# Four-stage attention and expert kernel: the last attention batch in its own bank with its projection behind the third chunk, channel attention one group later, and the last chunk in two halves

## The chip, the cores and the metric

The kernel runs on one core of a Trainium2 chip, in one launch. The metric is the device time of the whole launch in microseconds (us), lower is better. The engines are named as the profile names them: PE is TensorE, PEld its weight loads, DVE VectorE, ACT ScalarE, POOL GpSimd, SP SyncE, which here issues nearly all DMAs.

## The reference

`x` and `ctx` are (8, 128, 128) float32: 8 batches of 128 tokens and 128 channels. Four residual stages follow each other; `ln` is a layer norm without weights.

```python
x = x + channel_attention(ln(x), ctx, ctx)      # 4 heads of 32 channels, "global" + "local" scaling
x = x + expert_attention(ln(x))                 # 16 experts mix q, k, v; causal softmax; 16 experts project out
x = x + cross_attention(ctx, ln(x), ctx)        # 16 heads of 8: softmax(q k^T) v @ Wc.T + bc
x = x + expert_ffn(ln(x))                       # 8 experts, top 2, hidden 176, plus a shared branch of 352
```

The last stage, in which most of the change lies, is

```python
router = xf @ Wg;  top_logits, idx = top_k(router, 2);  w = scatter(softmax(top_logits))
h = silu(einsum('tc,ech->eth', xf, W1)) * einsum('tc,ech->eth', xf, W2)
y = einsum('eth,ehc,te->tc', h, W3, w) + (silu(xf @ Ws1) * (xf @ Ws2)) @ Ws3
```

## The kernel before, in words

Everything is laid out for 128 partitions. Each engine has one program in which a loop over a step number `s` calls small functions at steps written out by hand (`at_mix`, `at_score`, `at_att`, `at_tail`, `at_first`, `at_once`); within an engine the instructions run in exactly that order, and between engines semaphores order them. A PSUM bank is `PB[i]`, 128 x 512 float32; who may write a bank next is settled by waits too.

**Channel attention** works on halves of four batches. DVE computes scores and softmax, turns the heads (`turn_heads`, L1004) into a block-diagonal matrix `bd`, and PE multiplies it with the values (`attend_channels`, L1386, 8 products, 16 machine instructions). For the second half this lies inside the loop of the second stage: PE runs `turn_keys` (L1377), `spread` (L1472, the routing weights of four experts spread over the partitions) and `project` (L1488, four experts' q, k, v); DVE makes the scaled inputs `hm` (`scale_hidden`, L1099). After `attend_channels(1)` come DVE's statistics (L1011), ACT's `take_x1` (L594), and on SP the first loads of routing weights (L416), which wait for `att_ready`. ACT copies q, k, v out (L651, L652) before PE can turn them (L1498).

**Cross attention** (`at_att`) goes batch by batch: scores turned (L1596), exponential on ACT (L700), product with the values (`attend3`, L1609, 32 instructions into PB[3]), ACT takes it (`take_y`, L711), PE turns it (`turn_y`, L1616, into PB[3]), DVE divides (`divide`, L1162 and L1165), PE turns it back (`turn_divided`, L1622, PB[3]), ACT takes `yT` (L717), PE adds x and projects (`bring_x` L1631, `project_c` L1635, into PB[5]), DVE takes statistics (L1169), ACT takes x (`take_x3`, L721), POOL computes the reciprocal root (L488), DVE normalises (L881). All batches share PB[3], so `attend3(b)` waits for `yT_ready` of batch b-1.

**Router.** The 1024 tokens are two halves of 512. For the first half PE turns x (L1645) and multiplies with Wg (L1654) in PB[6]; DVE finds the two best (L1177 to L1196) and splits the weights into three bf16 parts (`three_parts`, L915 to L919); `turn_w` turns them (L1660, L1665); ACT takes them (`take_wT`, L757 and L759); SP stores them (L442) and loads them spread over partitions (L452) for the chunks that are not spread by PE.

**Expert chunks.** The 1760 hidden rows of the last stage (352 shared and 8 x 176) are 14 chunks of 128 rows, the last of 96, for each half of the tokens: k = 0 to 27. `up(k)` is six products of 512 columns (L1677: high and low parts of x and of two weights), ACT applies silu (L769, or L765 in place), DVE multiplies (`hidden`: L1219 for shared chunks, L1221 and L1223 for the three whose routing weights PE spreads by L1714, L1212 and L1215 for the others), ACT makes the high part (`high_hidden`, L746), POOL the low part (`split_hidden`, L533; the last two chunks on DVE, L1231), and `down(k)` is three products (L1733), the third of which needs the low part. Chunks 2, 3 and 4 are the ones spread by PE. `down(0)` is followed by eight instructions that add x (L1739). `result` (L773) and the store on SP (L457) end each half.

Around the change the hand-written places are: `attend_channels(1)` at step 16, before the step's `spread` and `project`; `attend3(7)`, `turn_y(7)`, `turn_divided(7)`, `bring_x(7)`, `project_c(7)` and `turn_w(0)` between `up(0)`, `up(1)` and `up(2)`; and the spread of chunk 2 inside `up(2)`.

## Time and profile before

| | us |
|---|---|
| median of 3 runs | 235.6 (233.77 to 235.94) |
| profiled execution, its own time | 234.7 |
| its span | 232.9 |
| PE busy | 209.8 (90%) |
| DVE busy | 166.4 (71%) |
| ACT busy | 112.0 (48%) |
| POOL busy | 95.1 (41%) |

The span runs from the first to the last instruction that the profile shows, and 1.8 us of the profiled execution's time lie around it. Times in the rows are in us from the span's start. The ends of matmuls are modelled, so durations of PE rows overlap; what a PE group costs is read here from the start of one group to the start of the next.

### The profile page before, as it was taken

The page shows a single profiled execution, that of the slowest core. Times are in us where ns is not written, and L with a number is a line of the kernel's source. Part 1 is how long each engine was busy: PE and PEld are TensorE (multiplying, and loading weights), DVE is VectorE, ACT ScalarE, POOL GpSimd, SP SyncE. Part 2 cuts the span into 40 slices and gives each one's busy share as a digit, 9 for nine tenths or more (in the row PEclk, how much of TensorE's full clock was granted, in tenths as well). Part 3 has the DMA queues.
Part 4 walks back from the last instruction along what each step waited for, and adds up shares of the span by engine and source line. Part 5 has one row for each costly group of instructions (what it writes and reads, how often), then busy time and mean ns, then how long its engine had stood idle before and what let it go on. Part 6 is the DMA issues. An engine that isn't in the chain of part 4 may idle for free.

```text
span 232.9 us, 5017 instructions
## 1 busy us (share of the span) xinstructions
PE 209.8 (90%) x1784; PEld 176.6 (76%) x1785; DVE 166.4 (71%) x495; ACT 112.0 (48%) x259; POOL 95.1 (41%) x127
## 2 busy tenths in 40 slices
PE   0199867899999999999999999998899999999994
PEld 0156546899999999998779888876677887778871
DVE  3498798659979889967686787864865687267653
ACT  0424543232244554422355867778354645645552
POOL 7142300160076999920321021231345755647660
PEclk9999999999999999999999999999999999999998
DMA  5998000298089955030210000000022320144401
GB/s 181 354 413 245 3 6 0 85 298 161 28 245 260 270 146 146 14 80 0 57 37 3 3 0 3 0 4 0 3 91 57 127 91 3 66 166 156 135 24 45
DMA packets 19256, 23.33 MB, mean 100 GB/s; under 512 B 1792, under 2 KB 12192, under 8 KB 19104
## 3 DMA queue, kind: packets, MB, share of 16 engines
q1 hardware_dynamic: 18896, 22.94, 32.7%
q8 instruction: 14, 0.23, 0.4%
q10 hardware_dynamic: 336, 0.08, 0.2%
q14 instruction: 10, 0.08, 0.1%
HBM read 22.39 MB, written 0.62 MB: 99 GB/s over the span
## 4 chain that ended last, share of the span: by engine, by line
PE 80%; DVE 9%; ACT 3%; DMA 3%; issue 2%; ACTq 1%; POOL 0%; DVEq 0%
PE psum L1677 17%; PE psum L1488 17%; PE psum L1733 8%; PE psum L1531 6%; PE psum L1596 3%; PE psum L1569 3%; PE psum L1609 3%; DMA kv<-kv_dram 3%; PE psum L1386 2%; PE psum L1342 2%; PE psum L1506 1%; PE psum L1554 1%; PE psum L1616 1%; PE psum L1521 1%; PE psum L1582 1%
## 5 line engine op out<-in xcount | busy, mean ns | idle before, releaser
L488 POOL TENSOR_TENSOR rstd<-ve,m 128x1 f32<-128x1 f32 (+1 forms) x20 | 14.2, 712 | 94.0 <-DVE ve L872 93.9
L1488 PE MATMUL psum<-wqkv,hm 128*128 128x192 f32 x256 | 46.4, 328 | 0.0
L533 POOL TENSOR_TENSOR qs<-hm,qs 128x512 fp32r<-128x512 f32 (+1 forms) x26 | 33.9, 1305 | 22.5 <-ACT qs L746 22.4
L1488 PEld LDWEIGHTS psum<-wqkv,hm 128*128 128x128 f32 x256 | 41.1, 190 | 0.1
L1144 DVE TENSOR_REDUCE negm<-psum 128x8 f32<-128x1024 f32 x16 | 19.5, 1222 | 7.7 <-PE psum L1569 7.2
L1733 PE MATMUL psum<-qs,wdhi 128*128 128x512 f32 (+1 forms) x56 | 21.8, 401 | 0.1
L1212 DVE TENSOR_TENSOR hm<-hm,psum 128x512 f32<-128x512 f32 x19 | 13.0, 686 | 11.4 <-PE psum L1677 5.5
L1099 DVE TENSOR_TENSOR hm<-xn2T,exT 128x512 f32<-128x512 f32 x24 | 19.3, 805 | 0.1
L746 ACT ACTIVATE qs<-hm 128x512 fp32r<-128x512 f32 (+1 forms) x28 | 17.5, 625 | 3.9 <-DVE hm L1215 2.5
L700 ACT ACTIVATE exT<-psum 128x1024 f32<-128x1024 f32 x16 | 16.4, 1023 | 5.6 <-PE psum L1596 5.1
L765 ACT ACTIVATE psum<-psum 128x512 f32<-128x512 f32 x19 | 11.1, 582 | 16.3 <-PE psum L1677 16.1
L1531 PE MATMUL psum<-wo,mixT 128*128 128x128 f32 x128 | 15.7, 276 | 0.1
L1531 PEld LDWEIGHTS psum<-wo,mixT 128*128 128x128 f32 x128 | 15.0, 192 | 0.3 <-issue 0.2
L1215 DVE TENSOR_TENSOR hm<-hm,psum 128x512 f32<-128x512 f32 x19 | 13.0, 687 | 2.0
L1733 PEld LDWEIGHTS psum<-qs,wdhi 128*128 128x128 f32 (+1 forms) x56 | 10.5, 188 | 3.3 <-DVE qs L1231 0.9
L1131 DVE TENSOR_TENSOR mixT<-aT,rwm 128x1024 f32<-128x1024 f32 x8 | 10.8, 1350 | 2.8 <-issue 2.6
L1677 PE MATMUL psum<-x4hi,wahi 128*128 128x512 f32 (+1 forms) x28 | 12.0, 430 | 0.2
L1596 PE MATMUL psum<-qs,ks 32*128 32x128 f32 x128 | 10.5, 281 | 1.0 <-ACT qs L705 0.9
L1733 PE MATMUL psum<-qs,wdlo 128*128 128x512 f32 (+1 forms) x28 | 11.1, 397 | 0.0
L1677 PE MATMUL psum<-x4lo,wahi 128*128 128x512 f32 (+1 forms) x28 | 11.1, 396 | 0.0
L1677 PE MATMUL psum<-x4lo,wbhi 128*128 128x512 f32 (+1 forms) x28 | 11.0, 394 | 0.0
L1677 PE MATMUL psum<-x4hi,walo 128*128 128x512 f32 (+1 forms) x28 | 11.0, 394 | 0.0
(237 smaller groups left out, 488.2 us busy)
## 6 DMA issues: line engine op xcount, KB each, us to landing
exT<-rw_rows SPq DMA_DIRECT2D x24, 256.0 KB, 4.4
rwm<-rw_rows SPq DMA_DIRECT2D x16, 256.0 KB, 5.0
hm<-ww_rows SPq DMA_DIRECT2D x7, 256.0 KB, 3.2
wqkv<-wqkv_dram SPq DMA_DIRECT2D x1, 1536.0 KB, 10.6
hm<-ww_rows SPq DMA_DIRECT2D x4, 224.0 KB, 2.9
wa<-wa_dram SPq DMA_DIRECT2D x1, 880.0 KB, 13.3
wb<-wb_dram SPq DMA_DIRECT2D x1, 880.0 KB, 13.4
wdn<-wdn_dram SPq DMA_DIRECT2D x1, 832.0 KB, 15.0
```

The costliest lines, as they stand in the source:

```text
L488: nc.gpsimd.tensor_tensor(dst, src, m16[:, 0:src.shape[1]], ALU.pow).then_inc(signal, 1)
L533: return nc.gpsimd.tensor_tensor(dst, src, hi.bitcast(F32), ALU.subtract)
L700: nc.scalar.activation(exT[:, b % 2, 2 * p:2 * p + 2, :], turned_pair, ACT.Exp).then_inc(ex_ready, 1)
L746: nc.scalar.activation(hhi[0:n, k % 3, :], hid[0:n, k % 3, :], ACT.Copy).then_inc(hhi_ready, 1)
L1099: V.tensor_tensor(hm[:, b % 2, 4 * q:4 * q + 4, :], bc(xn2T[:, b, :], 1, 4), weights, ALU.mult).then_inc(hm_ready, 1)
L1144: V.tensor_reduce(negm[:, b % 2, 2 * p:2 * p + 2, :], score_pair.rearrange("p j (g k) -> p j g k", g=4), AX.X, ALU.max, negate=True).then_ ...
L1212: V.tensor_tensor(hid[:, k % 3, :], ww[:, r % 3, :], bank, ALU.mult).then_inc(prod_ready, 1)
L1488: last = mm(bank[:, 0:3 * HD], hm[:, b % 2, e, :], wqkv[:, e, :], start=(e == 0), stop=(e == E0 - 1))
L1531: last = mm(PB[5][:, 0:C], mixT[:, r, :], wo[:, r, :], start=(r == 0), stop=(r == E0 // 2 - 1))
L1596: last = mm(PB[turned_score_bank(j)][:, T * g:T * g + T], ks[quarter(j), b, g, :], qs[quarter(j), b, g, :], start=True, stop=True)
L1677: last = mm(bank[0:n, :], w[:, c0:c0 + n], x[:, cols4], start=(j == 0), stop=(j == 2))
L1733: last = mm(bank[:, :], w[0:n, ch, :], h[0:n, k % 3, :], start=(ch == 0 and j == 0), stop=(ch == NCH - 1 and j == 2))
```

## The change

It has three parts, with no change in what is computed.

1. **Channel attention.** `attend_channels(1)` moves on PE from step 16 to step 18, which puts it behind the step's `spread` and `project`.
2. **Last attention batch.** Batch 7 of the cross attention uses PB[6] in place of PB[3] for its product, its two turnings and their readers. `attend3(7)` waits for `rt_used` (the first router half has been read out of PB[6]) in place of `yT_ready` of batch 6; `turn_w(0)`, which also writes PB[6], gets a wait for `yT_ready` of batch 7. `bring_x(7)`, `project_c(7)` and `turn_w(0)` move behind `up(2)`. The spreading product of chunk 2 leaves `up(2)` and stands as `spread_first` behind `down(0)` and its x products, with a semaphore `first_spread` for which DVE's second multiplication of chunk 2 waits. On ACT the high part of chunk 0 moves behind silu of chunk 1, and `take_x3(7)` ahead of `take_wT(0)`.
3. **Last chunk.** Silu, multiplication and high part of k = 27 are done in a left and a right half of 256 columns; the left low part is on POOL (new), the right one on DVE behind the low part of k = 26; `down(26)` leaves its third product to `down(27)`, which is now five products: four of high parts by halves, the third product of 26, and two half products of low parts. On ACT the high part of k = 26 moves ahead of silu of k = 27.

PE around the channel attention. L1386 (L1433 in the changed kernel) is the attention, L1472/L1519 the spreading, L1488/L1535 the projection, L1377/L1424 the turning of keys. Before:

```order
94 L1377 MATMUL psum<-ident,ksp 128x128 x4
95 L1386 MATMUL psum<-exT 128x128 x8
96 L1472 MATMUL psum<-partsT,sel 128x128 x4
97 L1488 MATMUL psum<-wqkv,hm 128x192 x4
98 L1377 MATMUL psum<-ident,ksp 128x128 x4
```

The same place in the changed kernel:

```order
94 L1424 MATMUL psum<-ident,ksp 128x128 x4
95 L1519 MATMUL psum<-partsT,sel 128x128 x4
96 L1535 MATMUL psum<-wqkv,hm 128x192 x4
97 L1433 MATMUL psum<-exT 128x128 x8
98 L1424 MATMUL psum<-ident,ksp 128x128 x4
```

One spreading and one projection now stand ahead of the attention; nothing else moves there.

ACT around the last attention batch. `qs<-hm` is a high part, `hm<-psum` silu, `xr` take_x3, `yT` take_yT, `ysb` take_y. Before:

```order
182 L711 ACTIVATE ysb<-psum 128x512 [waits z_ps,pv_done]
183 L746 ACTIVATE qs<-hm 128x512 [waits hid_ready]
184 L769 ACTIVATE hm<-psum 128x512 [waits up_ready]
185 L721 ACTIVATE xr<-psum 128x128 [waits x3_stats]
186 L717 ACTIVATE yT<-psum 128x128 [waits c_ready,yT_ps]
187 L746 ACTIVATE qs<-hm 128x512 [waits hid_ready]
188 L757 ACTIVATE wwT<-psum 32x128 [waits wwT_ps,wT_ps]
189 L759 ACTIVATE wT<-psum 128x512
190 L721 ACTIVATE xr<-psum 128x128 [waits x3_stats]
```

In the changed kernel:

```order
182 L733 ACTIVATE ysb<-psum 128x512 [waits z_ps,pv_done]
183 L803 ACTIVATE hm<-psum 128x512 [waits up_ready]
184 L776 ACTIVATE qs<-hm 128x512 [waits hid_ready]
185 L743 ACTIVATE xr<-psum 128x128 [waits x3_stats]
186 L739 ACTIVATE yT<-psum 128x128 [waits c_ready,yT_ps]
187 L776 ACTIVATE qs<-hm 128x512 [waits hid_ready]
188 L743 ACTIVATE xr<-psum 128x128 [waits x3_stats]
189 L787 ACTIVATE wwT<-psum 32x128 [waits wwT_ps,wT_ps]
190 L789 ACTIVATE wT<-psum 128x512
```

The first high part changes places with the silu behind it, and the last x stands ahead of the two copies of the routing weights.

ACT at the end of the program, before:

```order
243 L746 ACTIVATE qs<-hm 128x512
244 L769 ACTIVATE hm<-psum 96x512
245 L746 ACTIVATE qs<-hm 128x512
246 L746 ACTIVATE qs<-hm 96x512
247 L773 ACTIVATE xna<-psum 128x512
```

And in the changed kernel:

```order
243 L776 ACTIVATE qs<-hm 128x512 x2
244 L800 ACTIVATE hm<-psum 96x256
245 L801 ACTIVATE hm<-psum 96x256
246 L772 ACTIVATE qs<-hm 96x256
247 L774 ACTIVATE qs<-hm 96x256
248 L807 ACTIVATE xna<-psum 128x512
```

The high part of k = 26 goes ahead of the silu of k = 27, and both steps of k = 27 are in halves.

The diff, cut to its core:

```diff
+            def split_left(k):
+                pool.wait_ge(hhi_half, 1)
+                pool.wait_ge(down_done, k - 2)
+                low_part(hlo[0:n, k % 3, LEFT], hid[0:n, k % 3, LEFT], hhi[0:n, k % 3, LEFT]).then_inc(hlo_half, 1)
...
-                nc.scalar.activation(ysb[:, :, :].rearrange("p g t -> p (g t)"), PB[3][:, :], ACT.Copy).then_inc(y_ready, 1)
+                nc.scalar.activation(ysb[:, :, :].rearrange("p g t -> p (g t)"), PB[y_bank(b)][:, :], ACT.Copy).then_inc(y_ready, 1)
...
+                if is_last(k):
+                    nc.scalar.activation(gated[0:n, k % 2, LEFT], PB[gate_bank(k)][0:n, LEFT], ACT.Silu).then_inc(gated_half, 1)
+                    nc.scalar.activation(gated[0:n, k % 2, RIGHT], PB[gate_bank(k)][0:n, RIGHT], ACT.Silu).then_inc(gated_ready, 1)
+                    return
...
+                if n_routed(k) == 1:
+                    dve.wait_ge(first_spread, 1)
                 V.tensor_tensor(hid[:, k % 3, :], hid[:, k % 3, :], PB[3 if n_routed(k) % 2 == 1 else 4][:, :], ALU.mult).then_inc(hid_ready, 1)
...
+                if is_last(k):
+                    V.tensor_tensor(hlo[0:n, k % 3, RIGHT], hid[0:n, k % 3, RIGHT], hhi[0:n, k % 3, RIGHT].bitcast(F32), ALU.subtract).then_inc(hlo_ready, 1)
+                    return
...
                 if b == 0:
                     pe.wait_ge(aT_ready, NB)
+                elif b == NB - 1:
+                    pe.wait_ge(rt_used, 1)
                 else:
                     pe.wait_ge(yT_ready, b)
...
             def turn_w(hf):
+                if hf == 0:
+                    pe.wait_ge(yT_ready, NB)
...
+                    pe.wait_ge(hhi_half, 1)
+                    part(wdhi, hhi, LEFT, False)
+                    part(wdlo, hhi, LEFT, False)
+                    pe.wait_ge(hhi_ready, k + 1)
+                    part(wdhi, hhi, RIGHT, False)
+                    part(wdlo, hhi, RIGHT, False)
+                    pe.wait_ge(hlo_ready, k)
+                    mm(bank[:, :], wdhi[0:128, ch - 1, :], hlo[0:128, (k - 1) % 3, :], start=False, stop=False).then_inc(down_done, 1)
+                    pe.wait_ge(hlo_half, 1)
+                    part(wdhi, hlo, LEFT, False)
+                    pe.wait_ge(hlo_ready, k + 1)
+                    part(wdhi, hlo, RIGHT, True).then_inc(down_done, 1)
+                    return
...
-                if s == at_once(16):
+                if s == at_once(18):
                     attend_channels(1)
...
-                    if s == at_att(b, 62):
+                    if s == at_last(b, 62, 73):
                         bring_x(b)
...
-                    if s == at_tail(hf, 128, 176):
+                    if s == at_tail(hf, 137, 176):
                         turn_w(hf)
+                if s == at_once(LAST_W):
+                    spread_first()
```

## Rows read from the trace of the kernel before

**Rows 1.** The page: busy time of each engine, and the chain that ended last.

```profile
PE 209.8 (90%) x1784; PEld 176.6 (76%) x1785; DVE 166.4 (71%) x495; ACT 112.0 (48%) x259; POOL 95.1 (41%) x127
PE 80%; DVE 9%; ACT 3%; DMA 3%; issue 2%; ACTq 1%; POOL 0%; DVEq 0%
```

**Rows 2.** Waits of PE, the one that is touched first: us in total, times, longest.

```profile
PE psum L1386 <- DVE exT L1004: 1.4, 1, 1.4
```

**Rows 3.** Timeline, 37 to 51 us: start, duration, engine, line [idle before <- releaser].

```profile
41.45 2.05 PE L1386 MATMUL psum<-exT 128*128 128x128 f32 x16 [1.38 <-DVE exT L1004]
43.34 0.39 PE L1472 MATMUL psum<-partsT,sel 128*128 128x128 bf16 x4
...
43.59 3.67 SPq L416 DMA_DIRECT2D exT<-rw_rows  x8
...
44.36 0.88 DVE L1011 BATCH_NORM_STATS2 st<-psum 128x6 f32<-128x128 f32 x4
...
44.91 0.60 PE L1377 MATMUL psum<-ident,ksp 128*128 128x128 f32 x4
...
47.68 0.29 ACT L652 ACTIVATE v<-psum 128x128 f32<-128x128 f32 x1
...
48.51 0.27 PE L1498 MATMUL psum<-ident,qk 128*64 128x128 f32 x1
...
50.19 0.68 DVE L1099 TENSOR_TENSOR hm<-xn2T,exT 128x512 f32<-128x512 f32 x1
```

**Rows 4.** Landing times of the second stage's routing-weight transfers (tile rw_rows).

```profile
DMA to landing us min/median/max: 1.8/4.5/8.1
```

**Rows 5.** Timeline, 162 to 174 us.

```profile
163.34 1.08 PE L1609 MATMUL psum<-exT,vm 128*32 128x128 f32 x32 [1.01 <-ACT yT L717]
...
166.40 1.30 POOL L533 TENSOR_TENSOR qs<-hm,qs 128x512 fp32r<-128x512 f32 x1
...
166.53 1.22 DVE L916 TENSOR_TENSOR ga<-rww,wparts 128x32 f32<-128x32 f32 x1
...
167.89 0.28 ACT L717 ACTIVATE yT<-psum 128x128 f32<-128x128 f32 x1
...
168.06 0.49 PE L1631 MATMUL psum<-xr,ident 128*128 128x128 f32 x2 [0.74 <-ACT xr L721]
...
170.68 0.47 PE L1677 MATMUL psum<-x4hi,wahi 128*128 128x512 f32 x1
...
172.15 0.39 PE L1714 MATMUL psum<-wT,selw 128*128 128x512 bf16 x1
...
172.21 0.69 DVE L1223 TENSOR_TENSOR hm<-hm,psum 128x512 f32<-128x512 f32 x1
...
172.81 0.34 DVE L881 TENSOR_SCALAR xnb<-xr,mv,rstd 128x128 f32<-128x128 f32 x1
...
173.87 0.48 PE L1677 MATMUL psum<-x4hi,wahi 128*128 128x512 f32 x1
```

**Rows 6.** Timeline of the end, 226 to 230 us.

```profile
226.40 0.60 ACT L769 ACTIVATE hm<-psum 96x512 f32<-96x512 f32 x1 [0.96 <-PE psum L1677]
...
227.10 0.68 DVE L1219 TENSOR_TENSOR hm<-hm,psum 96x512 f32<-96x512 f32 x1 [1.25 <-ACT hm L769]
...
227.70 1.50 DVE L1231 TENSOR_TENSOR qs<-hm,qs 128x512 fp32r<-128x512 f32 x2
227.81 0.63 ACT L746 ACTIVATE qs<-hm 96x512 fp32r<-96x512 f32 x1 [0.30 <-DVE hm L1219]
...
229.79 0.60 ACT L773 ACTIVATE xna<-psum 128x512 f32<-128x512 f32 x1 [1.35 <-PE psum L1733]
```

**Rows 7.** Timeline, 67 to 69 us: POOL's subtractions beside a DVE product.

```profile
67.58 0.45 POOL L533 TENSOR_TENSOR wdlo<-wdn,wdhi 128x128 fp32r<-128x128 f32 x1
67.58 1.53 DVE L1131 TENSOR_TENSOR mixT<-aT,rwm 128x1024 f32<-128x1024 f32 x1 [1.11 <-issue]
...
68.16 1.26 POOL L533 TENSOR_TENSOR walo<-wa,wahi 128x128 fp32r<-128x128 f32 x1
```

More of the change, by code:

```diff
@@ L39 @@
 W4 = 13
+LAST_W = 474
 SLOT = 8
@@ L262, in build @@
         wparts_ready = sem("wparts_ready"); wT_ps = sem("wT_ps"); wT_ready = sem("wT_ready")
-        up_ready = sem("up_ready"); gated_ready = sem("gated_ready"); prod_ready = sem("prod_ready")
+        up_ready = sem("up_ready"); first_spread = sem("first_spread"); gated_ready = sem("gated_ready"); prod_ready = sem("prod_ready")
         hid_ready = sem("hid_ready"); hhi_ready = sem("hhi_ready"); hlo_ready = sem("hlo_ready")
@@ L278, in chunk_rows, with is_last @@
             return min(128, RUP - 128 * ch)
+        LEFT, RIGHT = slice(0, 256), slice(256, 512)
+        def is_last(k):
+            return k == 2 * NCH - 1
         def is_routed(k):
@@ L321, in at_att, with at_last, y_bank @@
             return SLOT * (Q3 + 2 * b) + u - ATT_EARLY[b]
+        def at_last(b, u, v):
+            return at_att(b, v if b == NB - 1 else u)
+        def y_bank(b):
+            return 6 if b == NB - 1 else 3
         def at_once(u):
@@ L574, in _ @@
                     split_hidden(s // SLOT - F4 - 1)
+                if s == LAST - 1:
+                    split_left(2 * NCH - 1)
         @block.scalar
@@ L716, in take_yT @@
                     act.wait_ge(c_ready, b - 1)
-                nc.scalar.activation(yT[:, b % 2, :], PB[3][:, 0:T], ACT.Copy).then_inc(yT_ready, 1)
+                nc.scalar.activation(yT[:, b % 2, :], PB[y_bank(b)][:, 0:T], ACT.Copy).then_inc(yT_ready, 1)
             def take_x3(b):
@@ L742, in high_hidden @@
                 n = chunk_rows(k % NCH)
-                act.wait_ge(hid_ready, k + 1)
+                if is_last(k):
+                    act.wait_ge(hid_half, 1)
+                else:
+                    act.wait_ge(hid_ready, k + 1)
                 if k >= 3:
                     act.wait_ge(down_done, k - 2)
+                if is_last(k):
+                    nc.scalar.activation(hhi[0:n, k % 3, LEFT], hid[0:n, k % 3, LEFT], ACT.Copy).then_inc(hhi_half, 1)
+                    act.wait_ge(hid_ready, k + 1)
+                    nc.scalar.activation(hhi[0:n, k % 3, RIGHT], hid[0:n, k % 3, RIGHT], ACT.Copy).then_inc(hhi_ready, 1)
+                    return
                 nc.scalar.activation(hhi[0:n, k % 3, :], hid[0:n, k % 3, :], ACT.Copy).then_inc(hhi_ready, 1)
@@ L842, in _ @@
                 for k in range(2):
-                    if s == at_first(k, 8):
+                    if s == at_first(k, 17):
                         high_hidden(k)
-                if s % SLOT == 0 and 2 <= s // SLOT - F4 - 1 < 2 * NCH:
+                if s % SLOT == 0 and 2 <= s // SLOT - F4 - 1 < 2 * NCH and s // SLOT - F4 - 1 != 2 * NCH - 2:
                     high_hidden(s // SLOT - F4 - 1)
@@ L1160, in divide @@
                 dve.wait_ge(z_ps, b + 1)
-                bank = PB[3][:, :].rearrange("p (h c) -> p h c", c=32)
+                bank = PB[y_bank(b)][:, :].rearrange("p (h c) -> p h c", c=32)
                 link(V.reciprocal(ry[:, :], bank[:, :, D1]))
@@ L1608, in attend3 @@
                     for j in range(4):
-                        last = mm(PB[3][quarter(j), T * g:T * g + T], vm[:, b % 2, 4 * g + j, :], exT[:, b % 2, j, T * g:T * g + T], start=True, stop=True)
+                        last = mm(PB[y_bank(b)][quarter(j), T * g:T * g + T], vm[:, b % 2, 4 * g + j, :], exT[:, b % 2, j, T * g:T * g + T], start=True, stop=True)
                 last.then_inc(pv_done, 1)
@@ L1615, in turn_y @@
                 for g in range(4):
-                    last = tr(PB[3][:, T * g:T * g + T], ysb[:, g, :], ident[:, :])
+                    last = tr(PB[y_bank(b)][:, T * g:T * g + T], ysb[:, g, :], ident[:, :])
                 last.then_inc(z_ps, 1)
@@ L1703, in up @@
                 last = three(PB[up_bank(k)], wbhi, wblo)
-                if is_routed(k) and n_routed(k) <= BY_PE:
+                if is_routed(k) and 1 < n_routed(k) <= BY_PE:
                     r = n_routed(k)
-                    if r == 1:
-                        pe.wait_ge(yT_ready, NB)
                     if r == 2:
@@ L1716, in up, with spread_first @@
                 last.then_inc(up_ready, 1)
+            def spread_first():
+                k = routed_chunk(1)
+                pe.wait_ge(yT_ready, NB)
+                pe.wait_ge(wT_ready, 1)
+                mm(PB[3][:, :], selw[:, :, :].rearrange("p e j -> p (e j)")[:, 128 * (k - NSHARED):128 * (k - NSHARED) + 128],
+                   wT[:, 0:512], start=True, stop=True).then_inc(first_spread, 1)
             def down(k):
@@ L1722, in down, with part @@
                 bank = PB[5 if hf else 6]
+                if is_last(k):
+                    def part(w, h, half, stop):
+                        return mm(bank[:, half], w[0:n, ch, :], h[0:n, k % 3, half], start=False, stop=stop)
+                    pe.wait_ge(hhi_half, 1)
[10 more added lines that the diff above has]
+                    part(wdhi, hlo, RIGHT, True).then_inc(down_done, 1)
+                    return
                 pe.wait_ge(hhi_ready, k + 1)
```

21 lines of the change are left out of this document (17 added, 4 removed).

## The prediction

> **What bounds the kernel now.** I read the page first, then the list of waits of PE, then the timeline around each wait that the change touches, and last the timeline of the end. The page shows PE busy for 90% of the span and carrying 80% of the chain that ended last [rows 1]. So the kernel is as long as PE's work plus the time in which PE stands still; a part of this change is worth something only where it removes standing time of PE, or shortens the last microseconds behind PE. No instruction of weight is removed. In PE's list of waits the reader finds three that are touched: 1.4 us at the second channel attention [rows 2], 1.0 us at the last `attend3`, and 0.7 us at the last `bring_x` (the brackets of [rows 5]). The fourth place is the end: silu of the last chunk begins at 226.40 and the last copy out at 229.79 [rows 6], 3.39 us of which PE's own work is a minor part.
>
> The profiled execution took 234.7 us with a span of 232.9, so 1.8 us lie around the span. The median of the three runs is 235.6, 0.9 above the profiled one. I take the level between the two, 235.15, and subtract the gain from it.
>
> **Part 1, channel attention behind one group.** Before, PE stands still for 1.38 us until the turned heads are there, at 41.45, so it was free at 40.07 [rows 3]. What now comes first is one spreading and one projection; from 43.34, where they begin today, to 44.91, where the next turning of keys begins, they take 1.57 us [rows 3]. In the changed kernel they run from 40.07 to 41.64, when the heads have been ready for 0.2 us. The attention takes 43.34 - 41.45 = 1.89 us, so PE is through at 43.53 in place of 44.91: 1.38 us ahead.
>
> What could take it back is what waits for the attention, now 0.19 us later. That is SP's queue: its first eight loads of routing weights were issued from 43.59 on and would start near 43.8. The slowest landing of this kind took 8.1 us, the median 4.5 [rows 4]; the first use is at 50.19 on DVE [rows 3], near 48.9 in the changed kernel, and 43.8 + 4.5 = 48.3. I count nothing, and keep up to 0.5 us for it in the range. DVE's statistics began at 44.36, behind an `hm` that had to wait for the late spreading [rows 3]; with that spreading early they begin when the attention ends, near 43.6, so this chain moves by only 0.75 us. ACT's copy of v ends at 47.68 + 0.29 = 47.97 [rows 3] and lies on it: 47.2 then. PE wants it at 48.51 - 1.38 = 47.13 [rows 3]. That costs about 0.13 us. Behind this point PE is ahead and the other engines follow it, since it carries most of the chain. Value 1.25 us; bounds 0.6 (statistics and a late load both bite) and 1.4.
>
> **Part 2, own bank and later projection.** `attend3(7)` no longer waits for ACT's yT of batch 6. It stood still for 1.01 us until 163.34 [rows 5]; its other inputs are early, since the exponential of batch 7 is already finished. So it starts at 162.33. The turning of y behind it needs ACT's copy as before and moves along. The next wait is `bring_x(7)`, 0.74 us until 168.06 [rows 5]. With up(2) in front of it (six products; those of up(3) take 172.15 - 170.68 = 1.47 us [rows 5]), PE arrives 1.01 us earlier for up(2) and then at about 167.7. ACT's yT of batch 7 ended at 167.89 + 0.28 = 168.17 [rows 5]; it moves forward by the same 1.0 us, but the high part of chunk 0 (0.5 us from start to start) now stands in front of it, so it ends near 167.7. No standing time is left: 1.01 + 0.74 = 1.75 us ahead when `turn_w(0)` is done.
>
> Given back: (a) ACT's copies of the routing weights now stand behind the last x, which needs DVE's statistics of batch 7, which stand behind DVE's xnb of batch 6. POOL's low part of chunk 0, which ran from 166.40 to 167.70, falls at about 167.4 to 168.7 in the changed kernel, and DVE's xnb would meet it. What such a meeting costs is seen at 166.53: a DVE subtraction of 32 columns takes 1.22 us and ends with POOL's at 167.7 [rows 5]. In the other direction a POOL subtraction that takes 0.45 us alone takes 1.26 beside a long DVE product, and ends a little after it [rows 7]. So the two shut each other out for whole instructions. Then wT is ready near 170.2. The spreading of chunk 3 stands at 172.15 today [rows 5]; 1.75 us earlier, and without the spreading of chunk 2 (about 0.25 us) in front of it, it is wanted at 170.15, and waits about 0.1 us. (b) The spreading of chunk 2 is moved behind the x products, at the same PE cost. PE needs 173.87 - 172.15 = 1.72 us from the spreading of chunk 3 to up(4) [rows 5], so with wT at 170.2 `first_spread` comes near 172.0 and up(4) near 172.2, and DVE's second multiplication of chunk 2, at 172.21 today [rows 5], starts no earlier than today. Behind it stand one xnb (0.34) and the first multiplication of chunk 3 (0.69), which up(5) waits for: 172.2 + 0.69 + 0.34 + 0.69 [rows 5] = 173.9, wanted at 172.2 + 1.47 = 173.67. That is 0.25 us. Together 0.35 us. The loads of routing weights for chunk 5 start with wwT, which is only about 0.3 us earlier than today; they were there some 3 us before use. Value 1.75 - 0.35 = 1.4 us; bounds 0.7 (both give-backs at a whole POOL instruction less what overlaps) and 1.8.
>
> **Part 3, last chunk in halves.** Today the chain is silu 226.40, multiplication 227.10 to 227.78, high part 227.81 to 228.44, low part on DVE to 229.20, copy out 229.79 [rows 6]. ACT has 0.96 us of idle time before that silu [rows 6], in which the high part of 26 now runs, so silu still starts near 226.4. No row shows a 256-column form of these four operations. Its bounds are half and whole of the 512-column rows; I take 0.38 on ACT (between 0.28 for 128 columns [rows 5] and 0.60 for 512 [rows 6]), 0.42 on DVE and 0.73 on POOL (between 0.45 [rows 7] and 1.30 [rows 5]). Left: silu to 226.80, product 226.90 to 227.32, high part to 227.75, so POOL is ready to start its low part at 227.8. Right: product to 227.7, high part to 228.15. DVE's low part of 26 starts at 227.7 as today, and takes 0.69 us to 228.4.
>
> If POOL and DVE do not hinder each other, POOL is done at 228.55, DVE's right half at 228.8, and the copy out starts near 229.2: gain 0.6 us. If they do, as in rows 5 and 7, POOL begins at 228.4 when DVE's low part of 26 ends, and ends at 229.1; the right half follows to 229.4, or goes first with the same sum. Against 229.20 today [rows 6] that is 0.2 late, of which the half-width last product gives back 0.15. All three instructions read two tiles of SBUF, as those of rows 7 do, so I take the second: value +0.1 us (bounds -0.3 and +0.7).
>
> The Trainium skill says the same in general (SBUF — State Buffer, "SBUF: two separate sides"): the port pair shared by VectorE and GpSimd is an exclusive lock, held for a whole instruction by whichever started first, among others by a VectorE op with two SBUF inputs. By that rule the left half on POOL is worth nothing; without it part 3 would be worth 0.6.
>
> **Sum.** 1.25 + 1.4 + 0.1 = 2.75 us. On the profiled execution 234.7 - 2.75 = 231.95; on the level taken 235.15 - 2.75 = 232.4 us. That is 1.2%, and about 1% is what a measurement of this kernel can tell from no change.
>
> **Rivals.**
> - *The end pays too* (the exclusion does not bite, or POOL slips in before DVE's long one): +0.6 in place of +0.1, and part 2 without give-backs, 1.75. 1.25 + 1.75 + 0.6 = 3.6: 231.5 us. For it: the right half on DVE is short. Against: rows 5 and 7.
> - *The early gain is swallowed.* Part 1 moves 1.4 us on PE to a place where loads and DVE must come along; if the loads of 43.6 land at the slow end, or DVE does not keep up in a stage in which it is busy most of the time, part 1 is worth 0.2 and the total 1.7: 233.5 us. For it: slowest landing 8.1 us [rows 4]. Against: PE carries 80% of the chain [rows 1], and other engines are released by it.
> - *Slower: the exclusion cascades.* If POOL's low parts of chunks 0 and 1 each block DVE for a whole 1.3 us ahead of the last x, wT comes 2.6 us later than I have it, and PE stands at the spreading of chunk 3: part 2 is 1.4 - 2.6 = -1.2; with DVE two steps late at chunk 4 another 0.7, the end -0.3, part 1 only 0.6. Sum -1.6: 236.7 us. It decides from wT later than 172.15, where the spreading stands today [rows 5]. Against: the second low part needs the high part of chunk 1 and POOL's root of batch 7, both of which come behind the DVE work that it would have to block.
> - *It does not do what it says*: `attend3(7)` finds another late input (its wait on the reader of PB[6] or the values' copy). Then part 2 keeps only 0.74 of its 1.75: total 1.7, 233.4 us.
>
> **How the numbers follow.** Forecast (gain 2 to 3.2 us) 0.56; the end pays too 0.16; early gain swallowed 0.15; attend3 held 0.06; slower 0.07 (of it 0.03 by over 1%). Own bounds sum to 0.6 + 0.7 - 0.3 = 1.0 and 1.4 + 1.8 + 0.7 = 3.9 us; with the level uncertain by 0.5 either way that is 230.8 to 234.6, and 8 in 10 lie in 230.8 to 234.4. Faster by over 1% needs 2.4 us: most of the forecast and the first rival, 0.60. Within 1% takes the rest of the forecast and the two middle rivals, 0.37. Slower by over 1%: 0.03.
>
> **What would show it.** In the changed profile the PE wait before the channel attention is gone or under 0.2 us, and everything from 60 to 155 us stands 1.1 to 1.4 us earlier than before. `attend3` of batch 7 and the last `bring_x` wait for nothing; up(4) starts 1.3 to 1.7 us earlier still. DVE's second product of chunk 2 waits for the spread and up(5) waits slightly for DVE. At the end POOL's half low part is stretched or starts only with the end of DVE's low part of 26; from the last silu to the copy out it is about 3.3 us. The prediction is wrong if stages between 60 and 155 us are not shifted, if a new PE wait over 0.5 us appears between 168 and 180 us, or if the end is 0.5 us shorter.

## The result, and the profile after

| | before | after |
|---|---|---|
| median of 20 runs, us | 233.88 (232.61 to 236.08) | 230.46 (229.11 to 234.42) |
| profiled execution, its own time | 234.7 | 230.48 |
| its span | 232.9 | 228.7 |
| the turning of keys ahead of the attention (39.47 and 38.56) to the turning of q and k | 9.04 | 7.82 |
| `up(0)` to `up(4)` | 13.27 | 11.27 |
| `up(0)` to `up(6)` | 17.77 | 16.23 |
| `up(27)` to the last copy out | 4.97 | 4.79 |

The ratio of the times is 0.987 with a 95% interval of 0.9849 to 0.9891: 1.3% faster, which on 233.88 is 3.0 us (2.5 to 3.5). Forecast were a gain of 2.75 us and a time of 232.4 us. The gain lies inside that interval, the time was 1.9 us too high and the low end of the range, 230.8, missed by 0.34. Some executions of either kernel lie 1 to 4 us above the others, with a lower mean granted clock of TensorE (the last section shows such a stretch); an "undisturbed median" below is the median over the executions in which that mean was 0.996 or more.

The page of the changed kernel, the lines that answer to [rows 1]:

```profile
PE 210.0 (92%) x1788; PEld 177.3 (78%) x1788; DVE 166.6 (73%) x496; ACT 112.4 (49%) x261; POOL 96.3 (42%) x128
...
PE 83%; DVE 8%; ACT 4%; DMA 2%; issue 1%; ACTq 1%; POOL 0%
```

PE's busy time is the same within 0.2 us, the span 4.2 us shorter: what went is standing time. Its waits, of the changed kernel (us in total, times, longest):

```profile
PE psum L1371 <- DMA cx<-ctx_dram: 5.3, 1, 5.3
PE psum L1381 <- DVE xna L917: 4.4, 2, 3.5
PE psum L1474 <- DVE rw L945: 1.2, 1, 1.2
...
PE psum L1545 <- ACT v L674: 0.2, 1, 0.2
```

The wait for `exT` of [rows 2] is gone, and so are those for yT and xr in [rows 5]. One has come, 0.2 us for ACT's copy of v. A wait of 0.18 us that this list does not name is shown further down. The turning of keys from which the first distance is taken, before the change:

```profile
39.47 0.60 PE L1377 MATMUL psum<-ident,ksp 128*128 128x128 f32 x4
```

The timeline of the changed kernel around the channel attention (start, duration, engine, line, idle before and releaser), to be laid beside [rows 3]:

```profile
38.56 0.60 PE L1424 MATMUL psum<-ident,ksp 128*128 128x128 f32 x4
...
40.58 2.01 PE L1433 MATMUL psum<-exT 128*128 128x128 f32 x16
...
42.43 0.60 PE L1424 MATMUL psum<-ident,ksp 128*128 128x128 f32 x4
42.63 0.89 DVE L1047 BATCH_NORM_STATS2 st<-psum 128x6 f32<-128x128 f32 x4 [0.83 <-PE psum L1433]
...
45.95 0.29 ACT L674 ACTIVATE v<-psum 128x128 f32<-128x128 f32 x1
...
46.38 0.27 PE L1545 MATMUL psum<-ident,qk 128*64 128x128 f32 x1 [0.19 <-ACT v L674]
```

The attention carries no bracket any more, and DVE's statistics begin as soon as it ends. The turning of q and k is 7.82 us behind this turning of keys (38.56) where it was 9.04 us behind it before. This launch also reached that turning at 38.56 where the one before reached it at 39.47, ahead of any changed instruction; over all profiled executions of this study it lies between 37.55 and 39.47. So 0.91 of the 4.2 us belong to the two launches and not to the change; it shows in PE's wait for xna in the first 25 us, 5.6 us before and 4.4 now, in code that is the same in both.

The stage of the last batch in the changed kernel, to be laid beside [rows 5]:

```profile
163.85 0.27 PE L1671 MATMUL psum<-ident,yq 128*128 128x128 f32 x1
...
163.87 0.48 PE L1728 MATMUL psum<-x4hi,wahi 128*128 128x512 f32 x1
...
165.24 1.29 POOL L547 TENSOR_TENSOR qs<-hm,qs 128x512 fp32r<-128x512 f32 x1 [1.52 <-ACT qs L776]
...
165.38 0.49 PE L1680 MATMUL psum<-xr,ident 128*128 128x128 f32 x2
...
165.44 1.18 DVE L917 TENSOR_SCALAR xnb<-xr,mv,rstd 128x128 f32<-128x128 f32 x1
...
167.19 0.57 ACT L789 ACTIVATE wT<-psum 128x512 bf16<-128x512 bf16 x1
...
167.48 0.39 PE L1728 MATMUL psum<-x4hi,wblo 128*128 128x512 f32 x1
...
167.90 0.38 PE L1763 MATMUL psum<-wT,selw 128*128 128x512 bf16 x1
...
169.72 0.38 PE L1771 MATMUL psum<-wT,selw 128*128 128x512 bf16 x1
...
169.74 0.58 PE L1728 MATMUL psum<-x4hi,wahi 128*128 128x512 f32 x1
...
170.20 0.69 DVE L1267 TENSOR_TENSOR hm<-hm,psum 128x512 f32<-128x512 f32 x1 [1.24 <-PE psum L1771]
...
170.81 0.34 DVE L917 TENSOR_SCALAR xnb<-xr,mv,rstd 128x128 f32<-128x128 f32 x1
...
171.06 0.68 DVE L1263 TENSOR_TENSOR hm<-hm,psum 128x512 f32<-128x512 f32 x1
...
171.84 0.47 PE L1728 MATMUL psum<-x4hi,wahi 128*128 128x512 f32 x1
```

`bring_x(7)` (L1680) starts 1.51 us behind `up(2)` (163.87) with no wait. xnb of batch 6 takes 1.18 us beside POOL's subtraction where 0.34 is its time alone, as forecast. PE did wait for wT, for 0.18 us: the spreading of chunk 3 (L1763) starts 0.42 us behind the product ahead of it (167.48), where before it started 0.24 us behind it (171.91 and 172.15), and it starts 0.14 us behind the end of ACT's copy of wT. In eight other profiled executions the first spreading product behind this copy starts the same 0.14 us behind its end; in the remaining five the record of that product is missing. What PE gives back beyond that is at `up(5)`: it starts 2.10 us behind `up(4)`, where before it was 1.53 us, since DVE's second multiplication of chunk 2 (L1267) waits for `spread_first` (L1771), and the first of chunk 3 (L1263) stands behind it. Before, the turning L1622 (L1671 in the changed kernel) was the last product ahead of the wait of `bring_x(7)`, whose start is at 168.06 in [rows 5]:

```profile
167.04 0.27 PE L1622 MATMUL psum<-ident,yq 128*128 128x128 f32 x1
```

The end of the changed kernel, to be laid beside [rows 6]:

```profile
222.45 0.36 ACT L800 ACTIVATE hm<-psum 96x256 f32<-96x256 f32 x1
...
223.58 0.68 DVE L1278 TENSOR_TENSOR qs<-hm,qs 128x512 fp32r<-128x512 f32 x1
...
223.86 1.00 POOL L547 TENSOR_TENSOR qs<-hm,qs 96x256 fp32r<-96x256 f32 x1 [1.03 <-ACT qs L772]
...
224.40 0.75 DVE L1276 TENSOR_TENSOR qs<-hm,qs 96x256 fp32r<-96x256 f32 x1
...
224.92 0.67 PE L1782 MATMUL psum<-qs,wdhi 96*128 96x256 f32 x2
225.62 0.60 ACT L807 ACTIVATE xna<-psum 128x512 f32<-128x512 f32 x1 [1.51 <-PE psum L1782]
```

From the last silu to the copy out it is 3.17 us, before 3.39. The left low part overlaps DVE's low part of 26 by 0.40 us, takes 1.00 us, and the right half on DVE takes 0.75 us.

The four distances add up: 1.22 at the attention, nothing from there to `up(0)` (112.09 us in both), 1.54 to `up(6)`, 0.18 at the end, together 2.94 us of change; with the 0.91 of the start and 0.32 between `up(6)` and `up(27)` (46.45 and 46.13 us; the other profiled executions have 46.10 to 46.38) this is 4.17 of the 4.2 us between the two spans.

### The profile page after: what moved, and what is told of

Read it like the earlier page. It is cut to its first block, busy times and chain, and to the rows that moved or that the text cites. A ratio compares the mean times of both kernels' runs of the same rounds, so it can differ in the third digit from the quotient of the medians.

```text
span 228.7 us, 5030 instructions
## 1 busy us (share of the span) xinstructions
PE 210.0 (92%) x1788; PEld 177.3 (78%) x1788; DVE 166.6 (73%) x496; ACT 112.4 (49%) x261; POOL 96.3 (42%) x128
## 4 chain that ended last, share of the span: by engine, by line
PE 83%; DVE 8%; ACT 4%; DMA 2%; issue 1%; ACTq 1%; POOL 0%
PE psum L1535 17%; PE psum L1728 17%; PE psum L1809 8%; PE psum L1578 6%; PE psum L1643 3%; PE psum L1616 3%; PE psum L1658 3%; DMA kv<-kv_dram 2%; PE psum L1389 2%; PE psum L1433 2%; PE psum L1553 1%; PE psum L1601 1%; PE psum L1665 1%; PE psum L1568 1%; PE psum L1629 1%
## 5 line engine op out<-in xcount | busy, mean ns | idle before, releaser
L1535 PE MATMUL psum<-wqkv,hm 128*128 128x192 f32 x256 | 46.4, 328 | 0.0
L547 POOL TENSOR_TENSOR qs<-hm,qs 128x512 fp32r<-128x512 f32 (+2 forms) x27 | 34.9, 1292 | 23.7 <-ACT qs L776 22.7
L1535 PEld LDWEIGHTS psum<-wqkv,hm 128*128 128x128 f32 x256 | 41.1, 190 | 0.1
L1809 PE MATMUL psum<-qs,wdhi 128*128 128x512 f32 (+1 forms) x53 | 20.4, 395 | 0.0
L795 ACT ACTIVATE psum<-psum 128x512 f32<-128x512 f32 x19 | 11.1, 582 | 17.3 <-PE psum L1728 17.2
L776 ACT ACTIVATE qs<-hm 128x512 fp32r<-128x512 f32 (+1 forms) x27 | 16.9, 626 | 3.9 <-DVE hm L1267 2.0
L1809 PEld LDWEIGHTS psum<-qs,wdhi 128*128 128x128 f32 (+1 forms) x53 | 10.0, 188 | 2.3
L1728 PE MATMUL psum<-x4hi,wblo 128*128 128x512 f32 (+1 forms) x28 | 11.0, 393 | 0.0
```

Source lines behind the costliest of these rows:

```text
L547: return nc.gpsimd.tensor_tensor(dst, src, hi.bitcast(F32), ALU.subtract)
L776: nc.scalar.activation(hhi[0:n, k % 3, :], hid[0:n, k % 3, :], ACT.Copy).then_inc(hhi_ready, 1)
L1535: last = mm(bank[:, 0:3 * HD], hm[:, b % 2, e, :], wqkv[:, e, :], start=(e == 0), stop=(e == E0 - 1))
L1728: last = mm(bank[0:n, :], w[:, c0:c0 + n], x[:, cols4], start=(j == 0), stop=(j == 2))
L1809: last = mm(bank[:, :], w[0:n, ch, :], h[0:n, k % 3, :], start=(ch == 0 and j == 0), stop=(ch == NCH - 1 and j == 2))
```

## The experiments

Each run is compared by the distances of the table above, since they leave the launch's start out, and where it was timed, also by the ratio to the kernel before. The undisturbed median of the kernel before is 233.19 us (24 executions beside the first four experiments), that of the changed one 230.17 (13 executions, those of the result).

**Each part alone.** The first puts `attend_channels(1)` at step 18 in the kernel before and changes nothing else.

```diff
-                if s == at_once(16):
+                if s == at_once(18):
                     attend_channels(1)
```

> The kernel before with part 1 alone (channel attention behind one spreading and projection). I read three distances on PE: from the third last turning of keys to the first turning of q and k (9.04 us before, 7.82 with the whole change), from up(0) to up(6) (17.77 and 16.23), and from up(27) to the last copy out (4.97 and 4.79). My theory, that each part only removes PE's own standing time: first distance 7.8, the two others as before, time 1.2 us (0.5%) below the kernel before. Rival, that the early gain is swallowed by later stages unless the rest of the change is there: first distance 7.8, but the stretch between turning q and k and up(0), 112.09 us in both kernels, is longer by up to 1.2, and the time is the same.

Measured: 9.04 became 7.82, the end stayed at 4.98. In the profiled execution the granted clock fell ahead of `up(0)` (last section): from q and k to `up(0)` it is 114.19 us and to `up(6)` another 18.66, so its distances alone do not rule the rival out. The times do: ratio 0.9943 (0.9911 to 0.9975), undisturbed median 231.98, 1.21 below. The theory held.

The second is part 2 alone: the changed kernel with the attention back at step 16 and the halves off.

```diff
-            return k == 2 * NCH - 1
+            return False
...
-                if s == at_once(18):
+                if s == at_once(16):
                     attend_channels(1)
```

> The kernel before with part 2 alone (own bank, later projection, later spreading of chunk 2, order on ACT). My theory: up(0) to up(6) 16.2 us as in the whole change, the first distance 9.0 and the last 5.0 as before, time 1.5 us (0.65%) below the kernel before. Rival, parts lean on each other: up(0) to up(6) above 16.6.

Measured: `up(0)` to `up(6)` 16.23, the other distances as before. Ratio 0.9965 (0.9928 to 1.0003); undisturbed median 231.68, 1.51 below.

The third is part 3 alone: PB[3], `bring_x(7)`, `turn_w(0)`, the spread of chunk 2 and the high part of chunk 0 as before, the halves on.

> The kernel before with part 3 alone (last chunk in halves, left low part on POOL). My theory, that the exclusion between POOL and DVE eats the halves: up(27) to the copy out 4.8 us against 4.97, the time within 0.1% of before. Rival, that the halves pay and only the profiled execution hid it: up(27) to the copy out 4.4 or less, time 0.25% lower.

Measured: the end 4.80, elsewhere 9.04 and 17.80. Ratio 1.0007 (0.9964 to 1.0049); undisturbed median 232.95, 0.24 below. Each part changes its own distance and, but for the fall of the clock in the first run, no other, and the undisturbed medians add: 1.21 + 1.51 + 0.24 = 2.96 us, against 233.19 - 230.17 = 3.02 for all three together. The intervals of the second and the third ratio include no change, and these medians are of 6 to 8 executions that spread by 0.8 to 1.6 us; what each part is worth rests on the distances, with which they agree.

**Part 2 taken apart.** The own bank without the moves, and the moves without the own bank. The edits are the two halves of part 2 of the diff: in the first, `bring_x(7)`, `project_c(7)`, `turn_w(0)`, `take_wT(0)`, the high part of chunk 0 and the spread of chunk 2 are where they were; in the second, `y_bank` returns 3 and `attend3(7)` waits for `yT_ready`:

```diff
-            return 6 if b == NB - 1 else 3
+            return 3
```

> The kernel before with the own bank alone: batch 7 in its own bank, its waits, nothing moved. My theory (1.01 us at attend3 and 0.74 us at bring_x are separate losses): attend3(7) waits for nothing, but bring_x(7) still waits 0.7 us for ACT, so up(0) to up(6) is about 16.8 (1.0 less than before). Rival, that ACT's chain behind attend3 sets the pace: then bring_x(7) waits about as much longer as attend3 waits less, and up(0) to up(6) stays above 17.4.

> The kernel before with the second half of part 2 alone: projection and turning of the weights behind up(2), spreading of chunk 2 later, order on ACT; but batch 7 stays in the common bank and waits for yT of batch 6. My theory: attend3(7) waits 1.0 us as before, bring_x(7) for nothing, and up(0) to up(6) is about 17.1 (0.74 less than 17.77, perhaps nothing given back, since PE arrives later). Rival, the own bank is what makes the move pay: 17.6 or more.

Measured: with the bank alone `attend3(7)` waits for nothing, and `bring_x(7)` still waits 0.7 us for xr. Its `up(0)` to `up(6)` was 18.00, on the rival's side; but between 160 and 165 us the granted clock was 0.79, and `up(0)` took 2.26 us in place of 1.46. Without those 0.80 it is 17.2, a gain of 0.57: 1.06 at `attend3(7)`, of which two new waits give back 0.23 and 0.25. The first is in `turn_w(0)`, from `up(1)` to `up(2)` (3.60 us in place of 3.37): PE comes 1 us earlier, but one of DVE's steps in splitting the weights (L948) takes 1.29 us beside POOL's low part (1.26), so the last part of the split weights is late. The second is at the spreading of chunk 2 (2.02 us from `up(2)` to `up(3)` in place of 1.76), which waits for wT. So the wait at `bring_x(7)` did not grow, as the theory says, and still 16.8 was too low. The lines of the bank alone:

```profile
166.41 1.29 DVE L948 TENSOR_TENSOR ga<-rww,wparts 128x32 f32<-128x32 f32 x1
...
168.09 0.27 PE L1705 MATMUL psum<-ident,rww 128*32 128x128 f32 x1
...
168.41 0.40 PE L1710 MATMUL psum<-identb,wparts 128*128 128x128 bf16 x4
```

Ratio 0.9972 (0.993 to 1.0014); undisturbed median 232.94 (7 executions from 231.75 to 233.5), 0.25 below, which is less than 0.57 and too coarse to decide. With the moves alone the wait of `attend3(7)` is back, that of `bring_x(7)` is gone, and `up(0)` to `up(6)` is 17.32: a gain of 0.45. Waits of PE in that kernel:

```profile
PE psum L1429 <- DVE exT L1036: 1.4, 1, 1.4
PE psum L1470 <- DVE rw L941: 1.2, 1, 1.2
PE psum L1652 <- ACT yT L737: 1.0, 1, 1.0
```

The two halves sum to 1.02 of the 1.54. The moves give back their 0.57 at `up(5)` with or without the bank; what is missing is, all but some 0.04, the 0.23 and 0.25 that the bank alone gives back and that the moves take away, since with them `turn_w(0)` and the spreading come later. Given the moves, the bank is worth its full 1.06 between `up(0)` and `up(1)`.

**What the give-back at `up(5)` hangs on.** First the spread of chunk 2 ahead of `down(0)`, behind the spreading of chunk 3:

```diff
-                if s == at_once(LAST_W):
-                    spread_first()
...
+                if s == SLOT * (F4 + 3):
+                    spread_first()
```

> The changed kernel with the spreading product of chunk 2 right behind that of chunk 3, ahead of down(0) and its x products. My theory: what is given back between up(4) and up(5) in the changed kernel (2.10 us from start to start against 1.53 before) is DVE coming late because its second product of chunk 2 waits for this spreading. DVE then starts it near 169 in place of 170.2, up(4) to up(5) is about 1.65, and up(0) to up(6) 15.8 in place of 16.23. Rival (PE waits at up(5) for something else, ACT or POOL): up(4) to up(5) stays at 2.1 and up(0) to up(6) at 16.2.

Measured: `up(4)` to `up(5)` 1.52, `up(0)` to `up(4)` 11.40 and to `up(6)` 15.90. In the timeline of this kernel DVE's two multiplications follow each other:

```profile
167.14 0.38 PE L1771 MATMUL psum<-wT,selw 128*128 128x512 bf16 x1
...
167.29 0.69 DVE L1263 TENSOR_TENSOR hm<-hm,psum 128x512 f32<-128x512 f32 x1 [1.04 <-ACT hm L803]
...
168.02 0.69 DVE L1267 TENSOR_TENSOR hm<-hm,psum 128x512 f32<-128x512 f32 x1
```

PE pays 0.12 us more up to `up(4)`, wins 0.58 at `up(5)` and gives 0.13 back up to `up(6)`. The theory held. Then the exclusion, the other candidate: the high part of chunk 0 on ACT back ahead of silu of chunk 1.

```diff
-                    if s == at_first(k, 17):
+                    if s == at_first(k, 8):
                         high_hidden(k)
```

> The changed kernel with one edit of part 2 undone: on ACT the high part of chunk 0 stands ahead of silu of chunk 1 again, as before. Theory (POOL's low part of chunk 0 shuts out DVE's xnb of batch 6): the low part starts about 0.6 us earlier and is over before xnb, which then takes 0.35 us instead of 1.18; wT comes earlier, but since the give-back at up(5) hangs on the spread of chunk 2 behind the x products and not on wT, up(4) to up(5) stays at 2.1 us. ACT's yT of batch 7 comes 0.5 us later, and bring_x(7) waits 0 to 0.3 us for it. up(0) to up(6) 16.2 to 16.5 us (16.23 in the changed kernel). Rival (the exclusion is what the give-back hangs on): up(4) to up(5) falls to 1.6 and up(0) to up(6) to 15.8.

```profile
163.02 1.30 POOL L547 TENSOR_TENSOR qs<-hm,qs 128x512 fp32r<-128x512 f32 x1
163.04 1.33 DVE L952 TENSOR_TENSOR ga<-rww,wparts 128x32 f32<-128x32 f32 x1
...
165.54 0.34 DVE L917 TENSOR_SCALAR xnb<-xr,mv,rstd 128x128 f32<-128x128 f32 x1
```

In this kernel xnb takes 0.34 us; the shut-out has moved to the subtraction of 32 columns, as in the kernel before. `up(4)` to `up(5)` is 2.10, `up(0)` to `up(6)` 16.24, so the rival is out: the give-back at `up(5)` does not hang on the exclusion. But PE feels the shut-out in either order. With xnb shut out (the changed kernel) it waits 0.18 us for wT at the spreading of chunk 3; here `up(3)` to `up(4)` is 3.33 in place of 3.51, and `up(2)` to `up(3)` 2.52 in place of 2.36, since `up(3)` (165.72) now stands right behind DVE's late multiplication of chunk 1, which ends at 165.62. The two cancel. No run here takes the shut-out away from both places; what the wait for the spread of chunk 2 costs in all is the 0.33 us of the run before.

**The end.** First the left low part on DVE, ahead of the right one, in place of POOL:

```diff
+                    V.tensor_tensor(hlo[0:n, k % 3, LEFT], hid[0:n, k % 3, LEFT], hhi[0:n, k % 3, LEFT].bitcast(F32), ALU.subtract).then_inc(hlo_half, 1)
                     V.tensor_tensor(hlo[0:n, k % 3, RIGHT], hid[0:n, k % 3, RIGHT], hhi[0:n, k % 3, RIGHT].bitcast(F32), ALU.subtract).then_inc(hlo_ready, 1)
```

> The changed kernel with the left low part on DVE too, behind the low part of k = 26; POOL does nothing there. In the changed kernel POOL's half takes 1.00 us and DVE's right half 0.75, while both lie beside each other. My theory (they shut each other out for whole instructions): DVE does the two halves in 0.25 to 0.42 us each without stretching, the last ends 0.1 to 0.3 us earlier than now, and up(27) to the last copy out falls from 4.79 to about 4.6. Rival (POOL's half runs beside DVE and is only slow): the two halves one after the other on DVE end later, 4.79 becomes 4.9 or more.

Then the left low part and its product left out of the computation altogether:

> The changed kernel without the left low part of k = 27 at all: the subtraction and its product on PE are left out. This prices the exclusion: my theory says DVE's right half, 0.75 us in the changed kernel, is then about 0.4 us, and up(27) to the copy out about 4.35. Rival (DVE's right half is 0.75 us for its own reasons): it stays 0.75 and the distance falls by no more than 0.1, what the left product costs PE.

Measured: 4.81 us with it on DVE, where the two halves take 0.42 and 0.41, so nothing is stretched, but the last of them ends no earlier than with POOL: neither the 4.6 of the theory nor the 4.9 of the rival. And 4.47 us without it (4.35 expected), where the right half takes 0.42 too, so that the 0.75 is POOL's doing and not its own. These are the low parts on DVE in the first of the two kernels:

```profile
223.86 0.68 DVE L1277 TENSOR_TENSOR qs<-hm,qs 128x512 fp32r<-128x512 f32 x1
...
224.67 0.42 DVE L1274 TENSOR_TENSOR qs<-hm,qs 96x256 fp32r<-96x256 f32 x1
...
225.01 0.41 DVE L1275 TENSOR_TENSOR qs<-hm,qs 96x256 fp32r<-96x256 f32 x1
```

So POOL's half costs DVE 0.33 us (0.75 against 0.42), no less than DVE would need to do it itself (0.34 from start to start): moving it to POOL bought nothing. By the rule of the Trainium skill (SBUF — State Buffer, "SBUF: two separate sides") the pair of ports that VectorE and GpSimd share is held for a whole instruction; the trace agrees as far as the sum goes, which comes out as if the work stood in one queue.

**Around the attention.** ACT's widening of the marks (1.37 us at 44.05 in the changed kernel) moved off the way of the copies, to a later place:

```diff
-                if s == at_once(17):
-                    wide_marks()
...
                 if s == at_once(56):
                     gate_exp(1)
+                    wide_marks()
```

> The changed kernel with one more edit: ACT's widening of the marks (1.37 us at 44.05 in the changed kernel, ahead of the copies of keys, q, k and v) moves behind a later exponential. Theory (the copy of v is late only because of that instruction): the 0.19 us wait of PE for v goes, and from the third turning of keys to the turning of q and k it is 7.65 us instead of 7.82. Rival: v depends on DVE's statistics and take_x1 or on PE's own projection, and the distance stays at 7.8. Elsewhere unchanged: up(0) to up(6) 16.2, last up to last copy 4.8.

Measured: the wait for v is gone and the distance is 7.46, better than expected. But the next turning waits for DVE's xnb, which hang on the statistics, and stands only 0.07 us earlier (relative to the turning of keys ahead of the attention) than in the changed kernel; and in its new place it delays ACT's exponential of the causal softmax, for which DVE then waits 0.23 us, and DVE's routing behind it; from q and k to `up(0)` it is 112.72 us, 0.63 more. A net loss of 0.27. The theory was right on the wait and wrong on its worth: two chains end within 0.2 us of each other there.

Then the attention one group later still:

```diff
-                if s == at_once(18):
+                if s == at_once(26):
                     attend_channels(1)
```

> The changed kernel with the second channel attention another group later on PE, behind one more turning, spreading and projection. Theory (0.2 us of slack is all there was; DVE's statistics stand ahead of the next scaled inputs in DVE's order, so a later attention holds the projection after it): statistics start near 44.6 instead of 42.63, the next scaled input is ready near 46.6, and the third turning of keys to the turning of q and k is 9.4 to 9.9 us, as bad as or worse than before (9.04). The time is then 1.6 to 2 us above the changed kernel's. Rival (PE carries the chain, the others follow): it stays near 7.8 and the time does not move.

Measured: the distance, from the turning of keys that starts it in the other kernels, is 10.10 us, 2.28 more than at step 18 and 1.06 more than before the change. PE's new wait is for v:

```profile
PE psum L1545 <- ACT v L674: 2.2, 1, 2.2
```

The rival is out, and a later attention does hold PE; but the way is not the one of the theory. The next scaled input is ready at 46.80 us, and PE turns q and k only at 48.45: ACT's copy of v ends at 48.31, behind `take_x1`, which needs the statistics (44.70), behind the widening of the marks (1.37 us from 46.12) and two more copies. The price was too low as well: the time is 235.81 us, 5.3 above the changed kernel's profiled one, 2.3 of it in this distance and 3.3 in two stretches in which the clock fell (last section), less 0.2 by which this launch began earlier. Whether the marks moved away would make step 26 as good as step 18 was not run.

**A version better than both.** The early spread, timed:

> The changed kernel with one edit, now timed in five rounds: spread_first stands behind the spreading of chunk 3 and ahead of down(0), so DVE's second multiplication of chunk 2 does not wait for down(0) and its x products. Theory (the 0.33 us that one look showed between up(0) and up(6) is a true saving that nothing behind takes back): the ratio to the kernel before is 0.987 - 0.33 / 234 = 0.9856, 3.4 us below it in place of 3.0; up(4) to up(5) 1.5 us, up(0) to up(6) 15.9. Rival (given back behind up(6), or too small to stand out): the ratio is 0.987 or more, and up(6) to up(27) grows over 46.3 us.

Measured: ratio 0.9821 (0.977 to 0.9872), median 229.97 of 6 executions; `up(4)` to `up(5)` 1.51, `up(0)` to `up(6)` 15.85, `up(6)` to `up(27)` 46.15. It is faster than the kernel before beyond doubt. That it is faster than the changed kernel is shown by the distances (0.33 to 0.38 us), not by the ratios, whose intervals overlap.

## Why the prediction was right and wrong

- *The level.* This is the step that failed: "I take the level between the two, 235.15". Twenty runs of the kernel before have a median of 233.88, so the level was 1.27 us too high. The profiled execution, 234.7, was no neutral one: against the changed kernel's, 0.91 us of it lie at the start of the launch (the latest of all profiled executions) and 0.32 between `up(6)` and `up(27)`. The three runs, 233.77, 235.6 and 235.94, spread over more than 2 us, and their median lies 1.7 us above the median of 20. The uncertainty of 0.5 given to the level was less than the spread that the three runs themselves showed. With the 233.88 of twenty runs the same gain gives 231.13, inside the range. The rest of the 1.94 us is that medians of 20 differ by 3.42 us and the forecast had 2.75; the ratio, which gives 3.0, is nearer to it.
- *Part 1*: 1.25 forecast, 1.22 measured (with the part alone 1.22 and a median 1.21 lower). The wait for v was 0.19 where 0.13 was worked out. The median landing time was the right one to take for the loads; nothing waited for them.
- *Part 2*: 1.4 forecast, 1.54 measured. Both waits went. PE waited 0.18 us for wT where 0.1 was worked out, by the way that the prediction gives (xnb shut out by POOL). `up(4)` came 2.00 us earlier where 1.67 was worked out. The 0.33 are a matter of how a wait is priced: the prediction took the brackets, 1.01 and 0.74, and by start times `up(0)` to `up(1)` is 1.06 shorter, and `turn_divided(7)` is followed by the next product after 0.03 us in the changed kernel (163.85 and 163.87) where it was 1.02 before, so that this wait was worth 0.99. Its row before: The give-back at `up(5)` was 0.57 us where 0.25 was worked out, and that is the same 0.3 once more: `up(5)` waits for DVE, whose order I had right (spread, second multiplication, xnb, first multiplication), and a PE that comes earlier only waits longer there. The forecast puts `up(5)` at 173.9, and it came at 171.84, which with the 2.13 us that the launch and part 1 had already moved is 173.97. The remaining 0.11 lie between `up(5)` and `up(6)` (2.97 and 2.85 us), for which no term was made.
- *Part 3*: 0.1 forecast, 0.18 measured. The halves took 0.36 (silu) and 0.42 (high part) on ACT, 0.42 on DVE, and 1.00 on POOL (0.73 taken) with DVE's at 0.75. The exclusion was the right choice of the two; with the left low part left out the distance is 4.47, a gain of 0.5 as against the 0.6 worked out. The +0.1 did not follow from its own working, 0.2 late less 0.15, which is -0.05; DVE's last low part ended 0.05 earlier, counted from `up(27)`, and not 0.2 later. That +0.1 stands near 0.18 is in part luck.
- *The rivals.* "The end pays too" is out by the two runs on the end. "The early gain is swallowed" is out: 112.09 us in both kernels from q and k to `up(0)`. "The exclusion cascades" is out: one DVE instruction ahead of the last x was shut out, and it cost PE 0.18 us at wT. "`attend3` is held" is out: no wait.

## What to carry to other kernels

Where one engine carries over 80% of the chain, a wait of it can be priced by start-to-start distances of that engine; the brackets of the timeline were 0.05 and 0.25 us short of them here. The sums came out within 0.15 us in all three parts. The level from which they are subtracted has to be found as carefully, from several runs and from where in the profiled execution its own excess lies. An instruction that fills a wait is worth it only up to the next chain: at step 18 the attention left 0.2 us of waiting, one group later it left 2.2. And a product moved behind other work takes its reader's queue with it: ask whether the earliest place at which its inputs are ready is not better than the one at which PE is free.

## What the runs showed of the hardware

TensorE's granted clock halved within this kernel, in two places while PE had work. (In half of the profiles it also falls once PE's last product is done, 1.2 and 1.4 us behind its end in the two compared ones, where it costs nothing; their mean clock of 0.996 is this alone.) Behind the wait of 2.2 us in the run with the attention at step 26 (stretch, length, busy time of each engine; the number before the DMA share is the granted clock):

```profile
46.00:48.00 2.00, 0.24 (x2) 0.00 (x0) 1.43 (x6) 2.00 (x4) 1.01 (x1) 1.00 0.80 259
48.00:50.00 2.00, 1.55 (x11) 1.46 (x12) 1.43 (x6) 0.61 (x3) 1.01 (x2) 0.69 0.87 257
50.00:52.00 2.00, 2.00 (x8) 2.00 (x8) 1.29 (x2) 0.55 (x2) 1.98 (x4) 0.50 0.96 284
52.00:54.00 2.00, 2.00 (x14) 1.65 (x13) 0.03 (x1) 0.00 (x0) 0.15 (x1) 0.96 1.08 300
```

PE is busy for 0.24 of 2 us, and then works for some 3.4 us at 0.5, which is the 1.2 GHz level. By start times the waiting cost 2.3 us (10.10 against 7.82) and the slow stretch behind it another 1.7 (PE's lag behind the changed kernel grows from 2.07 to 3.75 us). A wait can so cost nearly twice what the list of waits says of it.

The second place is the stage ahead of `up(0)`. In the profiled execution with part 1 alone:

```profile
154.00:156.00 2.00, 1.35 (x14) 1.15 (x14) 1.89 (x11) 0.94 (x3) 1.82 (x3) 1.00 0.00 0
156.00:158.00 2.00, 2.00 (x40) 1.69 (x37) 0.91 (x7) 1.02 (x1) 0.00 (x0) 0.53 0.00 0
158.00:160.00 2.00, 2.00 (x19) 1.59 (x12) 0.00 (x0) 1.24 (x3) 0.00 (x0) 0.50 0.00 0
160.00:162.00 2.00, 2.00 (x9) 1.87 (x9) 1.16 (x6) 1.76 (x2) 0.55 (x1) 0.50 0.00 0
```

PE stood still for 0.65 us of the first two microseconds, as it does in the changed kernel, whose clock stayed at 1.00 in the same stage; here the 1.2 GHz level held until past 162 us and cost 2.1 us up to `up(0)` (114.19 in place of 112.09) and 0.9 behind it. The runs with the attention at step 26 and with the bank alone show it too, for 3.4 us each. It meets the same instructions in some executions and not in others; what sets it off there no run shows. With it this execution is 3.0 us off, as much as the whole change is worth.
